# Moving the low parts of the squared keys between the statistics and the normalization in VectorE's queue

## The reference, cut to what matters

```python
# cross attention part, x is first put through a layer norm
h = rmsnorm(layernorm(x)) * g_res @ W_in.T + b_in
s = linear scan along the rows of rmsnorm(ctx)[:, :512] * g_init      # each row decays what comes before it by a factor of about 0.001
x = x + h + s[patch index of each row]
# feed-forward part, y = layernorm(x), y_prev = y shifted down by one row
r = sigmoid((mu_r * y + (1 - mu_r) * y_prev) @ W_r.T)
k = (mu_k * y + (1 - mu_k) * y_prev) @ W_k.T
x = x + r * (square(relu(k)) @ W_v.T)
```

## Time and profile before

| what | value |
|---|---|
| median of 3 runs | 798.63 us (798.57 to 801.33) |
| the profiled execution's own time | 801.11 us |
| its span, first to last instruction | 799.5 us |
| TensorE busy | 760.9 us (95%) |
| VectorE busy | 588.3 us (74%) |
| ScalarE busy | 398.3 us (50%) |
| GpSimd busy | 201.8 us (25%) |
| mean granted TensorE clock | 0.984 |

### The profile page before, as it was taken

The page is one execution under the profiler, slowest core; times in us unless marked ns, Lnnn a source line. Parts: engine busy times, 40 slices in busy tenths (PEclk is TensorE's granted clock), DMA queues, the critical chain, the costliest instruction groups (busy, mean ns, idle before and its releaser), DMA issues.

```text
span 799.5 us, 10975 instructions
## 1 busy us (share of the span) xinstructions
PE 760.9 (95%) x3458; PEld 620.9 (78%) x3459; DVE 588.3 (74%) x1074; ACT 398.3 (50%) x649; POOL 201.8 (25%) x169
## 2 busy tenths in 40 slices
PE   4679999899999999999999999999999999999997
PEld 1467688787888878788888888888887888878876
DVE  6878978778596777869596786968778685878462
ACT  3226744454564535556454545645453564544750
POOL 6134231402323140232313032231403223140000
PEclk9598999999999999999999999999999999999999
DMA  8385071350806226080623507071341707131011
GB/s 304 123 237 121 26 194 56 86 166 15 236 1 170 81 67 182 14 236 0 162 88 86 164 34 216 0 190 60 102 148 40 210 0 199 52 87 33 1 53 53
DMA packets 44733, 85.80 MB, mean 107 GB/s; under 512 B 5104, under 2 KB 5104, under 8 KB 44688
## 3 DMA queue, kind: packets, MB, share of 16 engines
q1 hardware_dynamic: 30864, 63.02, 22.2%
q0 software_dynamic: 9216, 16.78, 12.8%
q10 hardware_dynamic: 4608, 5.51, 1.9%
HBM read 63.51 MB, written 21.79 MB: 107 GB/s over the span
## 4 chain that ended last, share of the span: by engine, by line
PE 57%; DVE 17%; DMA 8%; issue 8%; POOL 4%; ACT 3%; DVEq 0%; POOLq 0%; ACTq 0%
PE bank L442 19%; PE bank L443 18%; PE bank L444 18%; DMA ring<-s_rows,patch_now 7%; POOL ring L402 3%; DVE bn_a L850 2%; DVE bn_b L960 2%; PE bank L546 2%; DVE normed L973 2%; DVE xk_lo L821 2%; DVE ring L954 2%; DVE scratch L924 1%; DMA s_rows<-scanned 1%; DVE xr_lo L821 1%; DVE bn_c L868 1%
## 5 line engine op out<-in xcount | busy, mean ns | idle before, releaser
L402 POOL DMA_INDIRECT ring<-s_rows,patch_now x64 | 105.9, 1655 | 159.5 <-DMA s_rows<-scanned 128.8
L924 DVE SCALAR_TENSOR_TENSOR scratch<-turned,mus,scratch 128x512 f32<-128x512 f32 x128 | 94.6, 750 | 35.6 <-ACT scratch L682 22.0
L442 PE MATMUL bank<-wi_hi,xt_hi 128*128 128x512 f32 x256 | 103.4, 404 | 0.7 <-DVE wi_lo L821 0.7
L442 PE MATMUL bank<-xk_hi,wk_hi 128*128 128x512 f32 x256 | 100.1, 391 | 3.0 <-DVE xk_lo L821 3.0
L443 PE MATMUL bank<-wi_lo,xt_hi 128*128 128x512 f32 x256 | 101.8, 398 | 0.0
L444 PE MATMUL bank<-wi_hi,xt_lo 128*128 128x512 f32 x256 | 101.4, 396 | 0.0
L442 PE MATMUL bank<-wv_hi,xr_hi 128*128 128x512 f32 x240 | 95.9, 399 | 5.7 <-DVE xr_lo L821 5.5
L442 PE MATMUL bank<-wr_hi,xr_hi 128*128 128x512 f32 x256 | 99.7, 390 | 0.0
L443 PE MATMUL bank<-xk_lo,wk_hi 128*128 128x512 f32 x256 | 99.6, 389 | 0.0
L444 PE MATMUL bank<-xk_hi,wk_lo 128*128 128x512 f32 x256 | 99.6, 389 | 0.0
L444 PE MATMUL bank<-wr_hi,xr_lo 128*128 128x512 f32 x256 | 99.6, 389 | 0.0
(11 more groups left out here) (116 smaller groups left out, 1309.0 us busy)
## 6 DMA issues: line engine op xcount, KB each, us to landing
xt<-in_x_turned SPq DMA_DIRECT2D x16, 1024.0 KB, 10.5
ring<-in_x SPq DMA_DIRECT2D x16, 1024.0 KB, 13.1
out<-gate SPq DMA_DIRECT2D x64, 256.0 KB
ctx_rows<-in_ctx SPq DMA_DIRECT2D x16, 512.0 KB
s_rows<-scanned ACTq DMA_DIRECT2D x19, 256.0 KB, 2.1
gate<-in_L_xattn_W_in SPq DMA_DIRECT2D x1, 1024.0 KB, 7.5
turned<-in_L_ffn_W_r SPq DMA_DIRECT2D x1, 1024.0 KB, 16.9
ring<-s_rows,patch_now POOLq DMA_INDIRECT x64
```

Source lines behind the costliest of these rows:

```text
L402: pool.indirect_dma_start(ring[b.slot][:, t, :], None, s_rows[:, :], bass.IndirectOffsetOnAxis(ap=patch_now[:, t:t + 1], axis=0), compute_ ...
L442: nc.tensor.matmul(where, lhs_hi, rhs_hi, start=start, stop=False)
L924: nc.vector.scalar_tensor_tensor(scratch[:, 2 + i % 2, :], turned[:, c, 1:S + 1], mus[:, which, c:c + 1], scratch[:, i % 2, :], ALU.mult, ...
```

## The change

The helpers stay as they are; only the order of their calls in VectorE's `iteration` changes, for iterations 1 to 14. The four `bn_stats` of `stats_a(new)` come first, then the first `ka_low`, then `norm_b`, then the second `ka_low`, then the rest of `stats_a` and all of `stats_c`, then the third `ka_low`, `x_lo(new, 0)`, the fourth `ka_low`, `scan_input(new)`, `x_lo(new, 1)`. `u_low(new)` follows as before.

```diff
                 if new.exists(B):
-                    stats_a(new)
-                    stats_c(new)
+                    for t in range(T):
+                        statistics_a(new, t)
+                if b.exists(B):
+                    ka_low(b, 0)
                 if nxt.exists(B):
                     norm_b(nxt)
-                for m in range(C):
-                    if b.exists(B):
-                        ka_low(b, m)
-                    if new.exists(B):
-                        if m in (1, 2):
-                            x_lo(new, m - 1)
-                        if m == 2:
-                            scan_input(new)
+                if b.exists(B):
+                    ka_low(b, 1)
+                if new.exists(B):
+                    stats_a(new, T)
+                    stats_c(new)
+                if b.exists(B):
+                    ka_low(b, 2)
+                if new.exists(B):
+                    x_lo(new, 0)
+                if b.exists(B):
+                    ka_low(b, 3)
+                if new.exists(B):
+                    scan_input(new)
+                    x_lo(new, 1)
                 if is_last(nxt):
                     mixing(nxt, 0, C)
                 if new.exists(B):
```

## The result

The changed kernel takes 804.65 us (median of 7 runs, 804.03 to 805.72) against 799.74 us for the kernel before (7 runs, 798.04 to 802.74). The ratio is 1.0061, with a 95% interval of 1.0041 to 1.0081: slower by 0.6%, clear of no change. The forecast was 805.0. The profiled execution of the changed kernel took 805.55 us, with a span of 803.9 us.

The account below looks back on a forecast made before the run. TensorE sets the pace, 45.96 us per batch without waits. Iterations 2 to 13 give +6.2 and iteration 1 -0.9, together +5.3: 803.9 or 806.4 depending on the base, 805.0 taken, range 799.5 to 808.5.

Parts of the forecast that it names:

- steps 3 and 4: VectorE's queue tail: u_lo ends at K + 16.12, tile 2's weights load at K + 17.99, period 47.09 us, 1.13 more.
- K: The time at which TensorE starts a batch's key product; times after it are within one iteration.
- the 1.8: Sign against the prediction: wrong if tile 2's weights load sooner than 1.8 us behind u_lo.
- step 2: VectorE's third ka_low ends at K + 11.44, due 12.02; its lateness goes, except about 1.3 us in iteration 1.
- Deadline of K + 14.90: Latest end of u_lo at which TensorE's tile 2 loses nothing: K + 16.77 less the fixed distance of 1.87.
- What was to cost nothing: Earlier norm_b, v_c 5.2 us later with the patch copy (GpSimd idles 11.33 us), and iteration 14: no cost.
- The reading is not hidden: Denies the rival that TensorE's table reading is hidden, giving -9.2 us, 791.9 or 789.4; chance 0.08.
- `u_lo` is not earlier than replayed: Denies the rival that u_lo ends earlier, near K + 15.67, leaving the time within 0.5%; chance 0.16.
- the transfers don't lengthen the period: Denies the rival that the late scan delays transfers and third low part, up to 1 us, 808 to 812; chance 0.06.
- the 10.6 us: All that TensorE's steady iterations lose: 7.3 from batch 2 to 14 and 3.3 from batch 1 to 2.
- the second loss: TensorE idle between scan and tile 2, reading its table only after u_lo; issue pieces of 5.5 us in 12.
- 2.5 us open: The profiled execution took 2.5 us more than the median of three runs; whether this lies outside the waits was undecided.

Follow-up runs that it names:

- e1: Changed kernel with scan_input straight behind the third ka_low and u_low straight behind the fourth; 793.13 us, ratio 0.9915 to the kernel before.
- e2: Changed kernel, VectorE's order untouched, with TensorE's two table reads ahead of the scan's wait for u_lo; 791.24 us, ratio 0.9897 to the kernel before.
- e4: Changed kernel with the second x_lo moved behind u_low; 801.34 us, ratio 1.0026 to the kernel before.
- e7: Changed kernel with TensorE reading the table twice behind the scan's wait, the first result unused; 829.42 us, ratio 1.0387 to the kernel before.
- e10: Changed kernel with two extra ScalarE copies ahead of the store to s_rows; 806.51 us, ratio 1.0096 to the kernel before.
- e6: Kernel before, old order, with TensorE's two table reads ahead of the scan's wait; 800.40 us, ratio 1.0022 to the kernel before.
- e8: Kernel before with the table read first and two extra ScalarE copies ahead of the store to s_rows; 812.78 us, ratio 1.0174.
- e9: Changed kernel with the table read first and two extra ScalarE copies ahead of the store to s_rows; 795.93 us, ratio 0.9967 to the kernel before.

## Why the prediction was right, point by point

- **The period (steps 3 and 4).** `u_lo` at K + 16.12 forecast, K + 16.13 measured; tile 2's weights 1.87 behind it forecast, 1.77 to 1.98 measured; 12 periods 565.1 forecast, 565.00 measured. Iteration 13, outside the hardware loop, is the one with 1.77, just under the 1.8 that the prediction named as a sign against itself. The idle time of the matmuls before tile 2, forecast at about 0.8 us, is 0.72 to 0.93 in iterations 1 to 13; the Relus of ScalarE waited 29.1 us in 13 times for low parts before and 0.8 us once in the changed kernel. The late iterations of the trace before were miscounted: eight have 1.81 to 1.97 (1 to 5, 8, 10, 11), with the mean of 1.87, and iteration 13 has 1.74. e1, e2, e4 and e7 show that the cause is the one named: the loss vanishes when the table is read first though `u_lo` is as late, moves one for one with `u_lo`, and grows with a second reading.
- **The third low part (step 2).** Forecast to end at K + 11.44 where `v_b` is early: measured K + 11.38 to 11.63. Only iteration 1 still waits. Its `v_b` came at K + 5.02 instead of the 4.63 that I carried over from the trace before, so it took 48.69 us and not 48.4.
- **Deadline of K + 14.90.** In e1 the iterations with `u_lo` at K + 14.95 to 15.0 lose 0.00 to 0.05 us and those at K + 15.19 lose 0.15 and 0.18, where 0.29 would follow from the deadline. So it lies about 0.1 us too early. The cause is that from an undisturbed load of tile 2 the next K follows after 457.93 - 428.74 = 29.19 us, and from a late one after 29.10; the forecast period has this difference in it, the deadline has not.
- **What was to cost nothing.** The earlier normalization, GpSimd's later patch copy and iteration 14 show nothing: the period of iterations 5 to 13 is accounted for by `u_lo` and the reading. GpSimd's later `rs_c` was free in the changed kernel, but it is what e1 ran into.
- **The rivals.** The reading is not hidden, `u_lo` is not earlier than replayed, and the transfers don't lengthen the period beyond 47.19 us (e10). The Trainium skill, "Advanced Engine Details and Errata", section "Sequencer and Instruction Queues", has an engine instruction pushed into a queue, where it waits for its semaphore while the sequencer goes on. That doesn't fit this wait on TensorE: in the changed kernel the table's first register operation starts at 428.4 behind a `u_lo` that ends at 428.33, and in e2 it starts at K + 13.80, behind the wait for the fourth `ka_low`, which ends at K + 13.73, and is over ahead of `u_lo`. Why the queue is held is not told apart further. The prediction put it down to a wait that stands by itself or is computed from a register; but in the trace the wait belongs to the scan's first weight load, and while iterations 1 to 12 wait against a register's value, iteration 13, which waits against a constant, is held as well.
- **What was mis-sized.** The statement that the 10.6 us are all that an order of VectorE's queue could win, made of two losses, treats them as separate. For the changed kernel this did no harm, since there the loop has slack. For the kernel before it was wrong: the second loss alone can't be won (e6), and e8 supports the reason given: it lies inside a loop that is about as long as TensorE's work. The two edits are worth +5 us (new order alone), +1.5 us (table first alone) and -8 us (both); neither is a gain without the other.
- **The base.** Between the profiled execution and the median I had left 2.5 us open. The longer series of the kernel before has its median at 799.74 with a spread of 4.7 us, the changed kernel 1.7 us. So 805.0 was a choice between 803.9 and 806.4, and that it came within 0.35 us of the median is partly luck: the excess from batch 1 to 14 was 5.59 where 5.3 was forecast, and the place of K of batch 1 alone differs by 1.17 between the two profiled executions. Part of the spread of the former is the timing of transfers, on which the latter's period doesn't depend; that is argued from e8 and e10, not measured by itself. K of batch 0 also moves by up to 1.6 us among these executions (78.97 in e2, 80.52 in e3), whatever the order.

The best kernel of the study is e2: the new order with TensorE reading its table ahead of the scan's wait, 791.24 us, ratio 0.9897 to the kernel before.

## What to carry to other kernels

When an order is changed to bring one operand forward, write down for each operand that moves back by when its reader's queue must have it, and not only by when the reader's instruction is due: control work such as a table reading or a branch behind a wait makes the queue's deadline earlier, here by about 1.2 us. Put such control work ahead of the wait. And before two losses are added up, ask whether they lie in one loop; a gain on an engine that a loop already holds back is given back as another wait, and a cheap test of that is to lengthen the loop by a known piece.

## What the runs showed of the hardware

- Reading two numbers from SBUF into TensorE's queue, with their checks and the branch, takes 1.75 to 1.93 us from the end of the awaited instruction to the end of the branch in the hardware loop of the changed kernel, and 1.72 in iteration 13 outside it; a second reading adds 1.3 us (e7). Each load from the table takes 0.30 us and the branch 0.21 to 0.34.
- The wait of the scan's first weight load for `u_lo` also held the control instructions behind it in TensorE's queue: the table's reading began 0.05 to 0.06 us after `u_lo` ended, in 13 of 13 iterations of both kernels, also where that weight load itself ran only 1.6 to 1.8 us after `u_lo` (iterations 6, 7 and 12 before).
- Idle gaps of the matmuls of 0.72 to 0.93 us in every iteration (1.15 to 1.36 us between weight loads) left the granted clock at 1.00. Gaps of 2.1 to 2.2 us (e7) were followed in four iterations of twelve by 3.4 us at the 1.2 GHz level, which cost 1.66 us each; the other eight, with the same gap, kept 2.4 GHz. It was every third iteration (3, 6, 9 and 12). In iteration 1 a gap of 1.78 us was followed by the same fall (e10), and gaps of 1.89 (e9) and 2.33 us (e8) were not. So the length of the gap alone does not decide it; what does is open.
